# One-row products with the mask and the biases, against the same products over 128 rows

## The chip, the cores and the metric

The kernel runs on one core of one Trainium2 chip, in one launch. The metric is the device time in microseconds (us). Before the change three runs gave 4461.14, 4453.69 and 4463.28 us; their median is 4461.14 us. The cuts that a reader needs of a core are its engines, which run side by side and meet only at semaphores: TensorE (PE in the rows, its weight loads PEld), VectorE (DVE), ScalarE (ACT), GpSimd (POOL) and the DMA queue that SyncE feeds (SP).

## The reference, cut to what matters

The program computes four pairs of an attention and a feed-forward layer on x, of shape (16, 256, 128). The change touches the first attention, to a context of 64 rows a batch, and the routing in front of the experts in the last layer:

```python
# first attention: 16 heads of 64, to the context
sim = einsum(q, k) * scale
sim = where(mask, sim, -max)            # one mask value per batch and context row
x = x + softmax(sim) @ v @ Wout.T + b_out
...
# last layer: the route
route_prob = softmax(xf @ Ws + bs, axis=-1).T     # 8 experts
```

## The kernel before, in words

x is worked on in 32 tiles of 128 tokens, four tiles to a pass, eight passes.

The first attention is `cross_attention` (lines 117 to 469). The weights are folded in pairs first (`fold`, line 235), so that a pass needs, for its two batches, a matrix `g` (scores come straight from the normalised x) and a matrix `vo` (the output comes straight from the probabilities). `unit` (lines 248 and 255) makes these for the next pass, one of eight units per iteration. An iteration `j` is one tile and eight of its 16 heads, 64 in all. Its work on TensorE, in this fixed order: `scores(j)` on lines 270 and 272, a unit for the next pass, on slot 7 also `turn_x` (line 215), `turn_prob(j-2)` on line 282, and `mix(j-3)` on lines 294 and 296. Line 270 puts the mask into the bank of scores as the product of a row of ones and a row of mask values; line 272 adds the scores to it. Line 294, once per tile, puts the bias into the bank of the output in the same way; line 296 adds four products of probabilities and `vo`. Each of these f32 products is two weight loads and two matmuls in the trace, the mask's (bf16) is one of each.

VectorE does, in iteration `i`: `weigh(i-1)` (sum, reciprocal, multiply: lines 360, 361, 364), `soften(i)` (maximum, subtract: 355, 356), and on odd iterations the addition to x and its statistics (368, 371, 372). In slot 3 of a pass it also makes the roots for the next layer (lines 76 to 80), in slot 4 (6 in the first pass) it normalises x for the next pass (347). ScalarE copies the units (437), takes the exponential (447), copies the turned x once a pass (423) and the turned probabilities (443). Everything waits by counting semaphores; no planner is involved.

The route is in `attend_and_route` (lines 3072 to 3360). After the attention of a pass, ScalarE normalises it (`norm`, 3303), TensorE turns it (`turn_r`, 3192), ScalarE copies it (3337), and `route` forms, for each of four tiles, a product with `ws` of eight columns (3200) and adds the bias as a product of a row of ones and the row `bs` (3201). VectorE then lowers and weighs (3269 to 3278) and ScalarE takes the exponential (3341).

Of the kernel before, what the change touches and what calls it, by code (L numbers as in the profile page):

```python
# [16 lines left out]
BF16 = mybir.dt.bfloat16  # L17
# [6 lines left out]
BATCH, SEQ, DIM = 16, 256, 128  # L24
CTX = 64
# [6 lines left out]
GROUP = 8  # L32
# [84 lines left out]
def cross_attention(nc, x_all, ident, dram, s_all):  # L117
# [10 lines left out]
    with ExitStack() as ctx:  # L128
        def sb(name, shape, dt=F32):
            return ctx.enter_context(nc.sbuf_tensor("x_" + name, shape, dt))  # L130
# [3 lines left out]
        def sem(name):  # L134
# [8 lines left out]
        fold_v = sb("fold_v", [128, 2, PAIRS, DIM])  # L143
        b_out = sb("b_out", [1, DIM])
        ctx_t = sb("ctx_t", [128, BATCH * CTX])
        mask_in = sb("mask_in", [1, BATCH * CTX], U8)
        mask_f = sb("mask_f", [1, BATCH * CTX])
        mask_b = sb("mask_b", [1, BATCH, CTX], BF16)
        ones = sb("ones", [1, 128])
        ones_b = sb("ones_b", [1, 128], BF16)  # L150
        stats, mv, var = sb("stats", [128, TILES, 6]), sb("mv", [128, TILES, 2]), sb("var", [128, 3, TILES])
# [12 lines left out]
            sem(n) for n in ("w_k_in", "w_q_in", "ctx_in", "w_v_in", "w_out_in", "b_in", "mask_arrived"))  # L164
        consts, zeroed, mask_made, own_v = sem("consts"), sem("zeroed"), sem("mask_made"), sem("own_vector")
        folded, fold_made, unit_done, unit_made = sem("folded"), sem("fold_made"), sem("unit_done"), sem("unit_made")
# [11 lines left out]
        @block.sync  # L178
        def _(sp):
            def load_x(p):  # L180
                at = slice(PASS_TOK * p, PASS_TOK * p + PASS_TOK)
                sp.dma_start(x_all[:, at], dram["x"][:, at]).then_inc(x_in[p], 16)

            sp.dma_start(w_k[:, :, :], dram["x_Wk"]).then_inc(w_k_in, 16)
            for n in range(2):
                half = slice(64 * n, 64 * n + 64)
                sp.dma_start(w_q[half, :, n, :], dram["x_Wq"][half, :, :]).then_inc(w_q_in, 16)
            load_x(0)
            sp.dma_start(ctx_t[:, :], dram["ctx_t"]).then_inc(ctx_in, 16)
            sp.dma_start(mask_in[:, :], dram["mask"]).then_inc(mask_arrived, 16)  # L190
            sp.dma_start(w_v[:, :, :], dram["x_Wv"]).then_inc(w_v_in, 16)
            for n in range(2):
                half = slice(64 * n, 64 * n + 64)
                sp.dma_start(w_out[half, :, n, :], dram["x_Wout"][half, :, :]).then_inc(w_out_in, 16)
            sp.dma_start(b_out[:, :], dram["x_b"]).then_inc(b_in, 16)
            for p in range(1, PASSES):
                load_x(p)

        @block.gpsimd
        def _(pool):  # L200
            nc.gpsimd.memset(ones[:, :], 1.0).then_inc(consts, 1)
            nc.gpsimd.memset(ones_b[:, :], 1.0).then_inc(consts, 1)
            for w in (w_q, w_out):
                nc.gpsimd.memset(w[0:64, :, 1, :], 0.0).then_inc(zeroed, 1)
                nc.gpsimd.memset(w[64:128, :, 0, :], 0.0).then_inc(zeroed, 1)

        @block.tensor
        def _(pe):
# [49 lines left out]
            def scores(j):  # L258
# [10 lines left out]
                to = score_bank[j % 2]  # L269
                nc.tensor.matmul(to[:, :], ones_b[:, :], mask_b[:, 2 * p + b, :].unsqueeze(1).broadcast_to([1, GROUP, CTX]), start=True, stop=False)  # L270
                at = 128 * (t % PASS_TILES)
# [54 lines left out]
        def _(dve):  # L326
# [57 lines left out]
            dve.wait_ge(mask_made, 2)  # L384
            nc.vector.tensor_copy(mask_b[:, :, :], mask_f[:, :].rearrange("a (b c) -> a b c", c=CTX)).then_inc(mask_made, 1)
            take_stats(1)
# [2685 lines left out]
def attend_and_route(nc, x_all, ident, dram, out, prob, table, weights, w_in, x_kept, table_in, prob_in):  # L3072
# [10 lines left out]
    with ExitStack() as ctx:  # L3083
# [13 lines left out]
        ctx_t, ctx_rows = sb("ctx_t", [128, BATCH * CTX]), sb("ctx_rows", [CTX, BATCH, DIM])  # L3097
        ws, bs, ones = sb("ws", [128, EXPERTS]), sb("bs", [1, EXPERTS]), sb("ones", [1, 128])
        stats, mv = sb("stats", [128, 2, TILES, 6]), sb("mv", [128, 2, TILES, 2])
        var, shift = sb("var", [128, 2, 3, TILES]), sb("shift", [128, 2, TILES])  # L3100
        xn, xn_t = sb("xn", [128, 2, PASS_TOK]), sb("xn_t", [128, 2, PASS_TOK])
        proj_t = sb("proj_t", [128, 2, PASS_TOK])
# [44 lines left out]
        @block.gpsimd  # L3147
        def _(pool):
            nc.gpsimd.memset(ones[:, :], 1.0).then_inc(ones_set, 1)

        @block.tensor
        def _(pe):
# [42 lines left out]
            def route(p):  # L3195
                pe.wait_ge(rn_t_made, p + 1)
                pe.wait_ge(r_lowered, p)
                for t in range(PASS_TILES):
                    s = route_bank[:, EXPERTS * t:EXPERTS * t + EXPERTS]
                    nc.tensor.matmul(s, tile(rn_t[:, p % 2, :], t), ws[:, :], start=True, stop=False)  # L3200
                    last = nc.tensor.matmul(s, ones[:, :], bs[:, :], start=False, stop=True)
                last.then_inc(r_done, 1)

            pe.wait_ge(loaded, 64)
            pe.wait_ge(route_in, 32)
            pe.wait_ge(ones_set, 1)
            for i in range(PASSES + LAG + 1):
# [609 lines left out]
```

## Time and profile before

| | before |
|---|---|
| median of three runs | 4461.14 us |
| the profiled execution's own time | 4456.33 us |
| its span, first to last instruction | 4454.5 us |
| outside the span | 1.8 us |
| PE, DVE, ACT, POOL busy, share of the span | 89%, 80%, 66%, 50% |
| mean granted TensorE clock | 0.931 of full |

The span is from the first to the last instruction of the program. Busy shares are means over stages with different limits: the first attention is the first 309 us, the route a stretch of about 60 us near 4200 us. A matmul's end is modelled, so starts of matmuls are a better ruler than their durations. [...]

### The profile page before, as it was taken

Reading aid. Unit: us, or ns where it says so; the run is one execution under the profiler, and the core shown is the slowest. Engines: PE = TensorE matmul, PEld = TensorE weight load, DVE = VectorE, ACT = ScalarE, POOL = GpSimd, SP = SyncE. Lnnn points to the kernel's source line nnn. Section 1 sums busy time; section 2 is a strip of 40 time slices with the busy share of each in tenths; the row PEclk is TensorE's granted clock in tenths of the full one; section 3 lists DMA queues with packets and bytes.
Section 4 is the critical chain, followed back from the end, with each engine's and each line's share of the span. In section 5 each row is a group of like instructions: output and inputs, shape, how many; then the busy total and the mean of one; then the engine's idle time right before and its main releaser. Section 6 shows DMA issues by size and latency. Waiting matters only on the chain. (4 is left out here: it accounts for less than half of the span.)

```text
span 4454.5 us, 117888 instructions
## 1 busy us (share of the span) xinstructions
PE 3964.2 (89%) x43247; PEld 2386.8 (54%) x43247; DVE 3584.2 (80%) x8496; ACT 2960.2 (66%) x5496; POOL 2206.9 (50%) x1392
## 2 busy tenths in 40 slices
PE   8978999999999999999999999999999855737735
PEld 5644555555555555555555555555555533525534
DVE  6887999899998999989999899989999655356341
ACT  3425787787777777777787787777778545636402
POOL 0005666666666666666666666666666400130006
PEclk9989999999999999999999999999999966868658
DMA  1012232333233332233232332232323200000102
GB/s 43 1 40 65 66 68 64 83 68 69 65 69 82 69 70 65 65 84 70 65 68 64 83 73 64 64 85 65 70 64 68 50 15 12 1 5 18 72 7 37
DMA packets 188120, 251.24 MB, mean 56 GB/s; under 512 B 88676, under 2 KB 129382, under 8 KB 187366
## 3 DMA queue, kind: packets, MB, share of 16 engines
q1 hardware_dynamic: 182054, 240.47, 23.2%
q0 software_dynamic: 5632, 4.33, 0.7%
q8 instruction: 352, 5.77, 0.6%
q14 instruction: 82, 0.67, 0.0%
HBM read 41.65 MB, written 14.30 MB: 13 GB/s over the span
## 5 line engine op out<-in xcount | busy, mean ns | idle before, releaser
L1419 POOL TENSOR_TENSOR f_rot_a<-f_rot_a,f_rot_b 128x1024 f32<-128x1024 f32 x384 | 908.1, 2370 | 311.8 <-DVE f_rot_b L1160 206.6
L1427 POOL TENSOR_TENSOR f_rot_a<-f_rot_a,f_norm 128x1024 f32<-128x1024 f32 x384 | 731.3, 1905 | 648.5 <-DVE f_norm L1178 525.4
L844 PE MATMUL f_bank<-f_w_vo,f_xs_t 128*32 128x512 f32 x6144 | 815.8, 603 | 0.2
L1157 DVE TENSOR_TENSOR f_rot_a<-f_bank,f_rot 128x512 f32<-128x512 f32 x768 | 523.0, 682 | 76.2 <-ACT f_squares L1519 40.4
L1528 ACT ACTIVATE f_vo<-f_bank 128x512 f32<-128x512 f32 x768 | 458.6, 597 | 170.2 <-PE f_bank L844 162.6
L1519 ACT ACTIVATE f_squares<-f_bank 128x512 f32<-128x512 f32 x768 | 455.8, 594 | 113.1 <-PE f_bank L830 67.1
L1540 ACT ACTIVATE f_k_t<-f_bank 64x512 f32<-64x512 f32 x768 | 452.7, 589 | 102.7 <-PE f_bank L866 98.2
L1160 DVE TENSOR_TENSOR f_rot_b<-f_bank,f_rot 128x512 f32<-128x512 f32 x768 | 505.9, 674 | 0.0
L1433 POOL TENSOR_TENSOR f_prob<-f_score,f_stat 128x512 f32<-128x512 f32 x384 | 400.6, 1043 | 192.1 <-DVE f_stat L1210 187.7
L1164 DVE TENSOR_REDUCE f_sums<-f_squares 128x16 f32<-128x1024 f32 x384 | 464.5, 1210 | 4.7 <-ACT f_squares L1519 4.7
L876 PEld LDWEIGHTS f_bank<-f_k_t,f_q_t 128*32 128x32 f32 x12288 | 345.4, 110 | 179.4 <-issue 99.5
L900 PEld LDWEIGHTS f_bank<-f_vo_off,f_prob_t 128*32 128x32 f32 x6144 | 330.8, 110 | 167.3 <-issue 150.7
L830 PE MATMUL f_bank<-f_w_qk,f_xs_t 128*128 128x512 f32 x768 | 400.5, 603 | 22.2 <-DMA f_w_qk<-in_Wqk 7.9
L876 PE MATMUL f_bank<-f_k_t,f_q_t 128*32 128x128 f32 x12288 | 406.0, 273 | 1.2 <-ACT f_bank L1546 0.6
L900 PE MATMUL f_bank<-f_vo_off,f_prob_t 128*32 128x128 f32 x6144 | 406.8, 274 | 0.2
L900 PE MATMUL f_bank<-f_vo,f_prob_t 128*32 128x128 f32 x6144 | 406.8, 274 | 0.0
L836 PE MATMUL f_bank<-f_w_qk,f_xs_t 128*128 128x512 f32 x768 | 401.7, 605 | 0.7 <-DVE f_rot_b L1160 0.7
L1533 ACT ACTIVATE f_q_t<-f_bank 128x512 f32<-128x512 f32 x384 | 227.9, 594 | 260.2 <-PE f_bank L860 260.2
L900 PEld LDWEIGHTS f_bank<-f_vo,f_prob_t 128*32 128x32 f32 x6144 | 330.8, 110 | 0.0
L1206 DVE TENSOR_REDUCE f_stat<-f_score 128x8 f32<-128x512 f32 x384 | 259.9, 677 | 76.8 <-ACT f_score L1550 71.9
L866 PEld LDWEIGHTS f_bank<-ident,f_rot_a 128*128 128x128 f32 x1536 | 180.4, 141 | 217.7 <-issue 153.8
L1198 DVE TENSOR_REDUCE f_stat<-f_bank 128x8 f32<-128x512 f32 x384 | 257.7, 671 | 29.1 <-PE f_bank L876 23.6
(446 smaller groups left out, 7372.8 us busy)
## 6 DMA issues: line engine op xcount, KB each, us to landing
f_vo_off<-f_vo SPq DMA_DIRECT2D x1152, 128.0 KB, 2.3
f_vo_off<-f_vo SPq DMA_DIRECT2D x384, 64.0 KB, 2.0
f_w_qk<-in_Wqk SPq DMA_DIRECT2D x12, 512.0 KB, 5.3
f_vo_dram<-f_vo_pair SPq DMA_DIRECT2D x48, 128.0 KB, 1.8
f_x_shifted<-s_all SPq DMA_DIRECT2D x48, 128.0 KB
f_x_shifted<-s_all SPq DMA_DIRECT2D x48, 127.0 KB
f_w_vo<-f_vo_dram SPq DMA_DIRECT2D x10, 512.0 KB, 5.4
e_w<-in_e_W SPq DMA_DIRECT2D x2, 2048.0 KB, 12.7
```

The costliest lines, as they stand in the source:

```text
L836: nc.tensor.matmul(flat(Q), chunk_x(t), w_qk[:, 0, 512 * g:512 * g + 512], start=True, stop=True).then_inc(q_done, 1)
L844: done = nc.tensor.matmul(bank[V][32 * w:32 * w + 32, :], x[:, at:at + 32], w_vo[:, 4 * g:4 * g + 4, w // 2, :], start=True, stop=True)
L876: done = nc.tensor.matmul(bank[S][32 * w:32 * w + 32, 128 * b:128 * b + 128], q_t[:, g, 128 * b + 32 * w:128 * b + 32 * w + 32], k_t[:, :, ...
L900: done = nc.tensor.matmul(bank[Y][32 * w:32 * w + 32, 0:128], prob_t[:, g, 128 * b + 32 * w:128 * b + 32 * w + 32], source[:, g, 2 * (t % ...
L1157: nc.vector.tensor_tensor(rot_a[:, slot, n, :].rearrange("p (h d) -> p h d", h=GROUP), source, c_tab, ALU.mult)
L1160: nc.vector.tensor_tensor(rot_b[:, g, n, :].rearrange("p (h s d) -> p h s d", h=GROUP, s=2), swapped, s_tab, ALU.mult).then_inc((q_rotated ...
L1164: nc.vector.tensor_reduce(sums[:, g, :], squares[:, g, :, :].rearrange("p n (h d) -> p (n h) d", h=GROUP), AX_X, ALU.add).then_inc(lengths, 1)
L1419: nc.gpsimd.tensor_tensor(rot_a[:, slot, :, :], rot_a[:, slot, :, :], rot_b[:, g, :, :], ALU.add).then_inc(rot_summed, 1)
L1427: nc.gpsimd.tensor_tensor(heads, heads, over(norm[:, 16 * g:16 * g + 16], [128, 16, HEAD_DIM]), ALU.mult).then_inc(qk_normed, 1)
L1519: nc.scalar.activation(squares[:, g, n, :], flat((Q, K)[n]), ACT.Square).then_inc((q_squared, k_squared)[n], 1)
L1528: nc.scalar.activation(vo[:, g, 2 * (t % 2) + j, :], flat(V), ACT.Copy).then_inc((va_copied, vb_copied)[j], 1)
L1540: done = nc.scalar.activation(k_t[r:r + 64, n, 4 * g:4 * g + 4, at:at + 128], flat(T)[r:r + 64, :].rearrange("p (b n) -> p b n", b=4), ACT ...
```

## The change

The stationary row of ones and the moving row (mask, bias) become 128 rows. In the moving operand 127 of them are zero, so the product is the same. The zero rows are written once at the start of each stage, on GpSimd, and three waits are added for them: SyncE's before the load of `b_out`, VectorE's before the mask is cast, and TensorE's at the start of the last stage, which now waits for a copy of `bs` that GpSimd makes after its DMA.

```diff
-        b_out = sb("b_out", [1, DIM])
+        b_out = sb("b_out", [128, DIM])
-        mask_b = sb("mask_b", [1, BATCH, CTX], BF16)
-        ones = sb("ones", [1, 128])
-        ones_b = sb("ones_b", [1, 128], BF16)
+        mask_b = sb("mask_b", [128, BATCH, CTX], BF16)
+        ones = sb("ones", [128, 128])
+        ones_b = sb("ones_b", [128, 128], BF16)
...
-            sp.dma_start(b_out[:, :], dram["x_b"]).then_inc(b_in, 16)
+            sp.wait_ge(cleared, 1)
+            sp.dma_start(b_out[0:1, :], dram["x_b"]).then_inc(b_in, 16)
...
             nc.gpsimd.memset(ones_b[:, :], 1.0).then_inc(consts, 1)
+            pool.wait_ge(consts, 2)
             for w in (w_q, w_out):
                 nc.gpsimd.memset(w[0:64, :, 1, :], 0.0).then_inc(zeroed, 1)
                 nc.gpsimd.memset(w[64:128, :, 0, :], 0.0).then_inc(zeroed, 1)
+            pool.wait_ge(zeroed, 4)
+            nc.gpsimd.memset(b_out[:, :], 0.0).then_inc(cleared, 1)
+            pool.wait_ge(cleared, 1)
+            nc.gpsimd.memset(mask_b[:, :, :], 0.0).then_inc(cleared, 1)
...
-                nc.tensor.matmul(to[:, :], ones_b[:, :], mask_b[:, 2 * p + b, :].unsqueeze(1).broadcast_to([1, GROUP, CTX]), start=True, stop=False)
+                nc.tensor.matmul(to[:, :], ones_b[:, :], mask_b[:, 2 * p + b, :].unsqueeze(1).broadcast_to([128, GROUP, CTX]), start=True, stop=False)
...
+            dve.wait_ge(cleared, 2)
-            nc.vector.tensor_copy(mask_b[:, :, :], mask_f[:, :].rearrange("a (b c) -> a b c", c=CTX)).then_inc(mask_made, 1)
+            nc.vector.tensor_copy(mask_b[0:1, :, :], mask_f[:, :].rearrange("a (b c) -> a b c", c=CTX)).then_inc(mask_made, 1)
...
-        ws, bs, ones = sb("ws", [128, EXPERTS]), sb("bs", [1, EXPERTS]), sb("ones", [1, 128])
+        ws, bs, ones = sb("ws", [128, EXPERTS]), sb("bs", [1, EXPERTS]), sb("ones", [128, 128])
+        bias_rows, bias_set = sb("bias_rows", [128, EXPERTS]), sem("bias_set")
...
             nc.gpsimd.memset(ones[:, :], 1.0).then_inc(ones_set, 1)
+            nc.gpsimd.memset(bias_rows[:, :], 0.0).then_inc(bias_set, 1)
+            pool.wait_ge(bias_set, 1)
+            pool.wait_ge(route_in, 32)
+            nc.gpsimd.tensor_copy(bias_rows[0:1, :], bs[:, :]).then_inc(ones_set, 1)
...
-                    last = nc.tensor.matmul(s, ones[:, :], bs[:, :], start=False, stop=True)
+                    last = nc.tensor.matmul(s, ones[:, :], bias_rows[:, :], start=False, stop=True)
...
-            pe.wait_ge(ones_set, 1)
+            pe.wait_ge(ones_set, 2)
```

## Rows read from the trace of the kernel before

**Rows 1.** Busy time per engine by stage: us, busy (count) each, PEclk, DMA share, GB/s

```profile
0.00:309.00 309.00, 277.96 (x1472) 176.00 (x1472) 247.75 (x648) 118.62 (x209) 5.15 (x14) 0.98 0.06 16
4189.80:4248.40 58.60, 41.84 (x165) 38.71 (x164) 13.99 (x78) 15.23 (x39) 0.00 (x0) 0.50 0.14 45
```

**Rows 2.** VectorE's waits from 80 to 280 us: total us, times, longest

```profile
DVE x_stat L360 <- ACT x_score L447: 11.0, 18, 0.7
DVE x_stat L355 <- PE x_bank L272: 2.7, 11, 0.4
```

**Rows 3.** Timeline of TensorE's matmuls in the first attention: start us, duration us

```profile
273.15 0.63 PE L282 MATMUL x_bank<-ident,x_prob 128*128 128x128 f32 x4
...
275.21 0.38 PE L270 MATMUL x_bank<-x_mask_b,x_ones_b 1*128 1x512 bf16 x1
...
276.82 0.63 PE L282 MATMUL x_bank<-ident,x_prob 128*128 128x128 f32 x4 [0.17 <-ACT x_prob_t L443]
277.28 1.06 PE L296 MATMUL x_bank<-x_vo,x_prob_t 128*128 128x128 f32 x8
278.27 0.39 PE L270 MATMUL x_bank<-x_mask_b,x_ones_b 1*128 1x512 bf16 x1
```

**Rows 4.** The same stretch, weight loads

```profile
273.70 0.29 PEld L294 LDWEIGHTS x_bank<-x_b_out,x_ones 1*128 1x128 f32 x2 [0.17 <-issue]
...
275.52 0.30 PEld L272 LDWEIGHTS x_bank<-x_g,x_xn_t 128*128 128x128 f32 x2 [0.23 <-issue]
...
277.18 0.97 PEld L296 LDWEIGHTS x_bank<-x_vo,x_prob_t 128*128 128x128 f32 x8
```

**Rows 5.** Timeline of matmuls in the third attention, all of 128 rows

```profile
3799.26 0.22 PE L2307 MATMUL a_bank<-a_causal,ident_bf 128*128 128x128 bf16 x1
3799.32 0.75 PE L2306 MATMUL a_bank<-a_k,a_q 128*128 128x256 f32 x2
```

**Rows 6.** Timeline of matmuls at the start of two passes

```profile
235.78 0.38 PE L270 MATMUL x_bank<-x_mask_b,x_ones_b 1*128 1x512 bf16 x1 [0.41 <-ACT x_xn_t L423]
236.10 1.13 PE L272 MATMUL x_bank<-x_g,x_xn_t 128*128 128x512 f32 x2
237.06 0.61 PE L248 MATMUL x_bank<-x_ctx_t,x_fold_q 128*128 128x128 f32 x4
...
268.96 0.39 PE L270 MATMUL x_bank<-x_mask_b,x_ones_b 1*128 1x512 bf16 x1 [0.42 <-ACT x_xn_t L423]
```

**Rows 7.** Timeline about the end of the first pass, TensorE, then VectorE

```profile
63.60 0.66 PE L215 MATMUL x_bank<-ident,x_xn 128*128 128x128 f32 x4 [2.41 <-DVE x_xn L347]
...
70.28 0.69 DVE L355 TENSOR_REDUCE x_stat<-x_bank 128x8 f32<-128x512 f32 x1 [1.51 <-PE x_bank L272]
...
73.13 0.69 DVE L360 TENSOR_REDUCE x_stat<-x_score 128x8 f32<-128x512 f32 x1 [1.44 <-ACT x_score L447]
```

**Rows 8.** Busy time, columns as in Rows 1

```profile
65.50:72.40 6.90, 5.94 (x22) 4.17 (x21) 4.48 (x10) 2.02 (x4) 0.00 (x0) 0.51 0.00 0
```

**Rows 9.** Timeline of VectorE in the last iterations of the first attention

```profile
296.20 0.69 DVE L355 TENSOR_REDUCE x_stat<-x_bank 128x8 f32<-128x512 f32 x1 [1.02 <-PE x_bank L272]
...
307.05 0.29 DVE L368 TENSOR_TENSOR x_all<-x_all,x_bank 128x128 f32<-128x128 f32 x1 [2.08 <-PE x_bank L296]
```

**Rows 10.** VectorE's and ScalarE's waits from 4184 to 4250 us

```profile
DVE y_r_stat L3269 <- PE y_bank L3201: 37.3, 7, 6.4
ACT y_r_score L3341 <- DVE y_r_score L3270: 36.2, 8, 6.9
```

**Rows 11.** Timeline of matmuls in one pass of the route

```profile
4222.39 1.12 PE L3192 MATMUL y_bank<-ident,y_rn 128*128 128x128 f32 x4 [2.31 <-ACT y_rn L3303]
4223.30 0.44 PE L3200 MATMUL y_bank<-y_ws,y_rn_t 128*128 128x8 f32 x2
4223.66 0.59 PE L3201 MATMUL y_bank<-y_bs,y_ones 1*128 1x8 f32 x2
...
4226.80 0.59 PE L3201 MATMUL y_bank<-y_bs,y_ones 1*128 1x8 f32 x2
4229.70 0.69 PE L3192 MATMUL y_bank<-ident,y_rn 128*128 128x128 f32 x2 [2.31 <-ACT y_rn L3303]
```

**Rows 12.** Timeline at the start of the first attention

```profile
13.05 0.95 POOL L205 MEMSET x_w_out<- 64x1024 f32 x1
...
14.93 1.36 SPq L195 DMA_DIRECT2D x_b_out<-in_x_b  x1
...
23.15 0.68 DVE L385 CAST x_mask_b<-x_mask_f 1x1024 bf16<-1x1024 f32 x1
```

**Rows 13.** Timeline at the start of the last attention

```profile
4120.76 1.65 ACT L3303 ACTIVATE y_xn<-x_all,y_shift,y_var 128x128 f32<-128x128 f32 x4 [15.34 <-DMA y_ctx_rows<-in_ctx_rows]
...
4122.66 1.08 PE L3157 MATMUL y_bank<-ident,y_xn 128*128 128x128 f32 x4 [13.35 <-ACT y_xn L3303]
```

More of the change, by code:

```diff
@@ L164, in cross_attention @@
             sem(n) for n in ("w_k_in", "w_q_in", "ctx_in", "w_v_in", "w_out_in", "b_in", "mask_arrived"))
-        consts, zeroed, mask_made, own_v = sem("consts"), sem("zeroed"), sem("mask_made"), sem("own_vector")
+        consts, zeroed, mask_made, own_v, cleared = sem("consts"), sem("zeroed"), sem("mask_made"), sem("own_vector"), sem("cleared")
         folded, fold_made, unit_done, unit_made = sem("folded"), sem("fold_made"), sem("unit_done"), sem("unit_made")
```

## Prediction, on record before the changed kernel ran

> **What bounds the kernel now.** I read the busy time by stage first, since the change touches two stages only: the first attention, 309 us, and the route, 59 us [rows 1]. The reader is to see there that TensorE is the busiest engine in both, and that its granted clock is 0.98 in the one and 0.50 in the other. Busy is not bound, so the waits come next. In the first attention from 80 to 280 us VectorE waits 2.7 us for TensorE's scores and 11.0 us for ScalarE's exponential [rows 2]; the second wait is VectorE's own work coming back (subtract, exponential, sum: at most 0.7 us a time, 18 times), and TensorE has no part in it. TensorE in turn runs without a pause but one of 0.41 or 0.42 us a pass [rows 6]. So both are nearly full, and a pass takes 268.96 - 235.78 = 33.18 us [rows 6]. What a faster TensorE is worth there is what VectorE waits for it, and little more. In the route it is the other way round: VectorE waits 37.3 of 66 us for the last bias product, ScalarE 36.2 us for VectorE [rows 10], and TensorE in turn 2.31 us for ScalarE in a pass of 4229.70 - 4222.39 = 7.31 us [rows 11]. That is one closed chain (normalise, turn, route, lower, exponential, normalise), and whatever TensorE saves in it comes off the time.
>
> **What a one-row product costs.** Starts of matmuls are the ruler. With a bias product between line 282's four matmuls and the next mask product: 275.21 - 273.15 = 2.06 us. Without one: 278.27 - 276.82 = 1.45 us [rows 3]. So its two matmuls of 128 columns cost 0.61 us. Matmuls of 128 rows and 128 columns cost 0.11 us each: line 282's four take 277.28 - 276.82 = 0.46 us. Two would be 0.22 us, so 0.39 us is lost about each bias product. The weight loads show how: the load for line 294 and the one for line 272 behind the mask product both stand behind an idle stretch put down to issue (0.17 and 0.23 us), while line 296's load starts at 277.18, before its first matmul at 277.28 and while line 282's last is still running [rows 3, 4]. A load is hidden behind the matmul before it when both have 128 rows, and it is not when the number of rows changes. The mask product has the same loss: 0.31 us to line 272 (236.10 - 235.78) where 512 bf16 columns at 128 rows would take 4 x (3799.32 - 3799.26 = 0.06), some 0.22 us [rows 5, 6]; 0.10 us ahead of it (278.27 - 277.28 = 0.99 for eight matmuls, against 8 x 0.11); and 0.10 us in line 272, whose two matmuls take 237.06 - 236.10 = 0.96 us where the second alone, with its load hidden, is worth some 0.43. Together 0.30 us. That rows 5 is bf16 between f32 products shows that the type makes no pause.
>
> The saving on TensorE is then 8 x 0.30 + 4 x 0.39 = 3.96 us a pass. In the route six of the seven steps from 4223.30 to 4226.80 are (4226.80 - 4223.66) / 6 = 0.52 us a product. The turn's four cold matmuls take 0.91 us, 0.23 each, and at best the half-speed image of 0.11, 0.21; a product is two [rows 11]. So 0.52 becomes 0.42 to 0.46; I take 0.42, as the first of the four carries an unhidden load: 6 x 0.10 = 0.62 us a pass.
>
> [...]
>
> **The sum, against the profiled execution (4456.33 us, 4454.5 in its span).**
> - Route: eight passes, all in the chain, 8 x 0.62 = 5.0 us (bounds 8 x 0.4 and 8 x 0.7).
> - Steady passes: VectorE's wait for scores, 2.7 us, goes [rows 2]. Behind it VectorE has its own work and ScalarE's exponential, so the rest of the 3.96 us a pass turns into idle time of TensorE.
> - First two iterations: TensorE makes the scores that VectorE waits for, 2 x 0.30 = 0.6 us.
> - End of the first pass: the clock is at 0.51 [rows 8] and VectorE waits 1.51 us for line 272 and 1.44 us for an exponential held up behind a copy from TensorE [rows 7]. The mask product's share of that, at half speed, and the later small waits: 0.9 us.
> - Last pass: VectorE's 1.02 us goes, as a bias and a mask product lie ahead of it at half speed; and one bias product, 0.39 us, lies ahead of the final addition [rows 9]. Together 1.4 us.
>
> Sum 5.0 + 2.7 + 0.6 + 0.9 + 1.4 = 10.6 us.
>
> **What is given back.** TensorE's idle time grows from 0.4 us a pass to 0.42 + 3.96 - 0.52 = 3.9 us. Following the order of work, about 1.1 of it comes where line 296 waits for a copy behind the exponential and 2.3 us in one piece ahead of slot 0, where line 270 waits for the turned x. The trace has one such piece: TensorE idle for 2.41 us before the turn at 63.60, and then the clock at half for 6.9 us [rows 7, 8]. That fall cost VectorE 1.51 + 1.44 - 0.70 = 2.25 us. In the new passes a fall should cost less: TensorE has work from the start, so I take half of those 6.9 us; after 3.4 us at half speed it is 1.7 us late, of which 0.4 to 0.6 is slack, so 1.2 us. [...] Net 10.6 - 3.6 = 7.0 us.
>
> **What costs nothing.** The wider memsets of ones are of the same length per row. The two memsets added at the end of GpSimd's list start at 14.00; the nearest row is 0.95 us for 1024 f32 elements a row, so the larger ends by 15.5 at most, and the cast that waits for it is at 23.15 [rows 12]: cover 7.6 us. Queued behind SyncE's new wait are seven loads of x; it is met near 14.3, ahead of 14.93 when the queue comes to it. Without that cover it would cost at most the memset's 0.95 us, and a gain is excluded, since nothing starts sooner. In the last stage TensorE waits for a copy of eight numbers behind a small DMA issued just after `ctx_rows`, which landed by 4120.76, while TensorE's first matmul is at 4122.66 for ScalarE's sake [rows 13]: 1.9 us of cover. If `bs` landed late, the cost would be that of one small copy, under 0.4 us. I take 0 for all of these.
>
> **The rivals.**
> - Full gain: the clock doesn't fall, as the idle piece is split. For it: it rests at 1.00 through 200 us of passes. Against: the 2.41 us case. 10.6 us less.
> - More than that: zero rows or the shorter pauses keep the clock up at the end of the first pass as well (2 us), or lift it in the route, where the turn and the route take 5.0 of 7.31 us at half speed (4226.80 + 0.59 - 4222.39) and would take about 2 us less a pass [rows 11]. For it: TensorE is packed more densely. Against: half of the route's products have 128 rows already and the clock is 0.50 all through [rows 1]. 13 to 26 us less.
> - No change: the pause isn't set by the rows but by something else about these operands (a new region of memory), and stays. Against: line 282 to line 296 changes operands as well, without a pause [rows 3, 4]. 0 us. [...]
> - Slower: the clock falls in each of the six passes and costs what the first fall cost, 6 x 2.25 = 13.5 us, against a gain of 10.6: 2.9 us more. From five falls of that size it decides the sign.
>
> **How the numbers follow.** Chances: the forecast (one to five falls) 0.48, full gain 0.27, more 0.08, no change 0.10, slower 0.07. Predicted time 4461.14 - 7 = 4454 us. The forecast's own range is a gain of 4.8 to 9.4 us. Medians of three have moved within 10 us among equal runs, so I allow 4 us on either side of a gain of 0 to 14: 4443 to 4463. What a measurement of this kernel can tell from no change is about 0.2%, 8.9 us: the full gain passes it mostly (0.20), the larger always (0.08), the forecast now and then (0.12): faster 0.40. Slower than that needs falls beyond six: 0.04. Same 0.56.
>
> **What would show it.** Right: in the profile after, the step from line 270 to line 272 is 0.21 to 0.22 us, a bias product 0.22 us, a product of the route 0.42 to 0.46, with no idle stretch put down to issue before the loads of lines 272 and 294. VectorE's wait for line 272 in 80 to 280 us is near 0 where the clock is 1.00. TensorE's wait for line 423 is 2 us or more a pass. A pass of the route is 6.7 us. Wrong: unchanged steps (the rows don't matter); a pass of the first attention shorter than 32.6 us (VectorE wasn't the bound); a granted clock of 1.00 in all passes, or below 0.9 in all.

## The result, and the profile after

| | before | after |
|---|---|---|
| median of 20 runs each, in alternation on one chip | 4462.12 us | 4452.5 us |
| ratio after / before, 95% interval | | 0.9979 [0.9973, 0.9986] |
| the profiled execution's own time; its span | 4456.33; 4454.5 us | 4458.58; 4456.8 us |
| first attention, from the first mask product to the last normalised sum | 284.5 us | 277.9 us |
| route, from the first to the last product with `ws` | 56.5 us | 51.8 us |

The changed kernel is faster by 0.21%, with an interval of 0.14% to 0.27%: 6 to 12 us, where the forecast was 7 and 4454 us. One of the 20 executions after took 6802.6 us at a granted clock of 0.551 (a slow state); it is counted in the median and left out of the ratio. The profiled execution happens to be one of its slower ones, so its total says nothing, and its stages have to be compared one by one. The two stages that were changed are 6.7 and 4.7 us shorter. The span is 2.3 us longer all the same, so 13.7 us lie in stages whose instructions are the same. Outside the two stages the profiles of the twelve kernels here show 4113.5 us (the kernel before) to 4127.8 us, and the kernel after stands near the top with 4127.2. Whether the change costs anything there is not shown; the timed runs leave room for about 2 us of it, since the two stages gain 11.4 us and the medians 9.6.

The busy time by stage, with the columns of [rows 1], of the kernel after:

```profile
0.00:309.00 309.00, 247.71 (x1472) 174.15 (x1472) 249.68 (x658) 116.97 (x209) 6.78 (x17) 0.98 0.06 16
4193.50:4248.00 54.50, 36.38 (x165) 34.59 (x164) 14.02 (x78) 15.23 (x39) 0.00 (x0) 0.50 0.16 49
```

TensorE is busy for 30 us less in the first attention, with the same number of matmuls, and no longer leads VectorE. Its mean granted clock stands where it stood, at 0.98 and 0.50. The traces give it as 1.00 or 0.50 (in the kernel before 1.00 from 80 to 280 us, 0.50 from 68.0 to 72.4 us and in the route); a figure between is a mean over a stretch, and half speed below is a granted clock of 0.50. Now the starts of its matmuls, the ruler of the prediction:

```profile
259.87 0.60 PE L288 MATMUL x_bank<-ident,x_prob 128*128 128x128 f32 x4
260.31 0.39 PE L300 MATMUL x_bank<-x_b_out,x_ones 128*128 128x128 f32 x2
260.53 1.06 PE L302 MATMUL x_bank<-x_vo,x_prob_t 128*128 128x128 f32 x8
263.28 0.39 PE L276 MATMUL x_bank<-x_mask_b,x_ones_b 128*128 128x512 bf16 x1 [1.69 <-ACT x_xn_t L430]
263.51 1.02 PE L278 MATMUL x_bank<-x_g,x_xn_t 128*128 128x512 f32 x2
264.37 0.60 PE L288 MATMUL x_bank<-ident,x_prob 128*128 128x128 f32 x4
```

A bias product (line 300, before 294) takes 260.53 - 260.31 = 0.22 us from start to start, where it cost 0.61. A mask product (line 276, before 270) is 0.23 us ahead of its scores here and 0.21 or 0.22 in the other slots, where it was 0.31 to 0.32. The scores take 264.37 - 263.51 = 0.86 us, where they took 0.96 [rows 6]. The weight loads, against [rows 4]:

```profile
265.59 0.10 PEld L276 LDWEIGHTS x_bank<-x_mask_b,x_ones_b 128*128 128x128 bf16 x1
265.70 0.41 PEld L278 LDWEIGHTS x_bank<-x_g,x_xn_t 128*128 128x128 f32 x2
...
267.63 0.30 PEld L300 LDWEIGHTS x_bank<-x_b_out,x_ones 128*128 128x128 f32 x2
267.86 0.97 PEld L302 LDWEIGHTS x_bank<-x_vo,x_prob_t 128*128 128x128 f32 x8
```

Ahead of lines 278 and 302 the idle stretch put down to issue is gone: the load starts while the matmul before it runs (the mask product itself starts at 265.70, and in the same moment the weights of the scores begin to load). The starts of the loads say it for all of them. From 80 to 280 us of the kernel before, a load at a change of rows starts 198 to 203 ns behind the start of the 128-column matmul before it (313 behind the mask product of 512 columns) and 1 to 4 ns ahead of its own matmul; where the rows stay at 128 it starts 1 to 3 ns behind the start of the matmul before it and some 109 ns ahead of its own (medians). After the change the loads of lines 276, 278, 300 and 302 start 2 or 3 ns behind the start of the matmul before them. The waits from 80 to 280 us, against [rows 2]:

```profile
PE x_bank L288 <- ACT x_prob_t L450: 14.3, 16, 1.7
...
DVE x_stat L366 <- ACT x_score L454: 11.0, 18, 0.7
PE x_bank L276 <- ACT x_xn_t L430: 10.2, 6, 1.7
```

VectorE's wait for scores, 2.7 us in 11 pieces, is no longer listed. Its wait for the exponential is 11.0 us in 18 pieces of at most 0.7, as before. What TensorE saved has become its own waiting for ScalarE's two copies. And one pass of the route, against [rows 11], with VectorE's and ScalarE's waits from 4184 to 4250 us [rows 10]:

```profile
4224.93 0.43 PE L3212 MATMUL y_bank<-y_ws,y_rn_t 128*128 128x8 f32 x2
4225.21 0.57 PE L3213 MATMUL y_bank<-y_bias_rows,y_ones 128*128 128x8 f32 x2
4225.64 0.57 PE L3212 MATMUL y_bank<-y_ws,y_rn_t 128*128 128x8 f32 x2
...
4227.77 0.57 PE L3213 MATMUL y_bank<-y_bias_rows,y_ones 128*128 128x8 f32 x2
...
4230.65 1.11 PE L3204 MATMUL y_bank<-ident,y_rn 128*128 128x128 f32 x4 [2.31 <-ACT y_rn L3315]
4231.56 0.43 PE L3212 MATMUL y_bank<-y_ws,y_rn_t 128*128 128x8 f32 x2
```

```profile
DVE y_r_stat L3281 <- PE y_bank L3213: 32.5, 7, 5.7
ACT y_r_score L3353 <- DVE y_r_score L3282: 31.5, 8, 6.9
```

A product takes 0.43 us, a pass 4231.56 - 4224.93 = 6.63 us, and VectorE's and ScalarE's waits have shrunk by 4.8 and 4.7 us, by what the stage became shorter. The 2.31 us that TensorE waits for ScalarE are the same 2.31.

### The profile page after: what moved, and what is told of

Read it like the earlier page. It is cut to its first block and busy times, and to the rows that moved or that the text cites. A ratio compares the mean times of both kernels' runs of the same rounds, so it can differ in the third digit from the quotient of the medians.

```text
span 4456.8 us, 117896 instructions
## 1 busy us (share of the span) xinstructions
PE 3942.4 (88%) x43247; PEld 2391.9 (54%) x43247; DVE 3584.8 (80%) x8496; ACT 2958.5 (66%) x5496; POOL 2208.4 (50%) x1396
```

## The experiments

Medians are of 5 to 11 runs (20 for the kernel after), the kernel before ran in alternation with each on the same chip, and the ratio is to it. Steps are from the start of one matmul to that of the next, medians over many; the pass is that of the steady state.

| kernel | time, before on its chip | ratio, 95% interval | pass, first attention | pass, route |
|---|---|---|---|---|
| before | | | 33.18 us | 7.31 us |
| after | 4452.5, 4462.1 | 0.9979 [0.9973, 0.9986] | 32.55 | 6.63 |
| mask alone | 4456.0, 4461.2 | 0.9990 [0.9981, 0.9999] | 32.53 | 7.31 |
| bias alone | 4458.5, 4461.2 | 0.9995 [0.9986, 1.0004] | 32.78 to 32.80 | 7.31 |
| route alone | 4458.6, 4461.2 | 0.9992 [0.9983, 1.0001] | 33.18 | 6.63 |
| 64 rows | 4461.9, 4461.2 | 1.0002 [0.9993, 1.0011] | 33.18 | 7.31 |
| before, grouped | 4460.2, 4463.7 | 0.9992 [0.9982, 1.0001] | 33.20 | 6.73 |
| no mask | 4459.7, 4468.2 | 0.9981 [0.9972, 0.9990] | 32.51 | 6.64 |
| sums on GpSimd, after | 4462.3, 4468.2 | 0.9983 [0.9974, 0.9992] | 32.34 | 6.63 |
| sums on GpSimd, before | 4468.4, 4468.2 | 1.0002 [0.9993, 1.0011] | 33.00 | 7.31 |
| one bias product | 4447.5, 4468.2 | 0.9955 [0.9941, 0.9968] | 32.55 | 5.36 |
| both additions | 4444.1, 4463.7 | 0.9956 [0.9942, 0.9969] | 32.35 | 5.36 |

**Each part alone.** Three kernels keep all the memory and the waits of the change and differ only in the slices that the products read:

```diff
 mask alone:   ones[0:1, :], b_out[0:1, :]      ones[0:1, :], bias_rows[0:1, :]
 bias alone:   ones_b[0:1, :], mask_b[0:1, ...]  ones[0:1, :], bias_rows[0:1, :]
 route alone:  ones[0:1, :], b_out[0:1, :]      ones_b[0:1, :], mask_b[0:1, ...]
```

> The changed kernel, but only the mask product has 128 rows; the bias product of the first attention and that of the route are made over one row again. My theory (a weight load is hidden behind the matmul before it only when both have the same number of rows; VectorE bounds a steady pass of the first attention, the closed chain through TensorE bounds the route): step mask product to scores 0.215 us instead of 0.31, bias product still 0.6 us, TensorE saves 2.4 us a pass, of which VectorE's wait of 0.52 is worth anything, so a steady pass of 32.6 us as with all edits; the first attention ends 5 us earlier than before; the route's pass stays at 7.31 us. In all 4455 to 4458 against 4462 (ratio 0.9989). Rival (TensorE bounds the first attention, so all its savings come off the time): 8 x 2.4 = 19 us less, 4443.

> The changed kernel, but only the bias product of the first attention has 128 rows. My theory: TensorE saves 4 x 0.39 = 1.56 us a pass; as that is more than VectorE's wait of 0.52, a steady pass is also 32.6 to 32.7 us, so the mask's and the bias's savings overlap rather than add: 3.5 to 4.5 us off the first attention, nothing off the route, 4458 in all (ratio 0.9991). Rival (TensorE bounds): 12.5 us less, and the sum of this run's and the mask run's gains is the gain of the whole first attention.

> The changed kernel, but only the route's bias product has 128 rows. My theory: the first attention as before (pass 33.18 us), a pass of the route 6.64 us instead of 7.31, 5 us off the time: 4457 (ratio 0.9989). Rival (the gain of the whole change lies in the first attention alone): no change, 4462.

With the mask alone the step from line 302 to the mask product falls from 208 to 112 ns, the next from 315 to 216, the one within the scores from 533 to 429: 0.30 us together, as worked out. With the bias alone the steps from the turn through the bias to the second matmul of line 302 fall from 203, 213, 200 and 213 to 112 or less: 0.38 us, where 0.39 was worked out. Read so, each change of the number of rows slows the two matmuls behind it, by about 0.10 us each at a granted clock of 1.00 (three in all for the mask, whose product is a single matmul). In the route, at a granted clock of 0.50, the steps of 291, 235, 287 and 233 all become 213: 0.076 and 0.021 us behind a change, together the 0.10 of the forecast. Each part's stage moves, and the others don't. In the first attention the parts don't add up: 0.65 and 0.40 us a pass alone, 0.63 together. Either edit brings VectorE near its own bound, and the second finds little left. The bias alone was expected at 32.6 to 32.7 us and stays at 32.8, where VectorE still waits for scores, 0.8 us in 5 pieces from 80 to 280 us, at the start of slot 0. The medians are 5.2, 2.6 and 2.6 us under that of before, their sum 10.4, and the whole 9.6. The bias and the route alone gave less than was expected (4 and 5 us); their intervals hold that as well as 1, so the parts are told by their passes.

**How many rows, and how many changes.** Here the products run over 64 rows, 63 of them zero, in the first kernel. The second is the kernel before with the eight products of a pass of the route in another order: four with `ws`, then the four one-row ones. `s(t)` is the slice that was `s`. In that order the output comes out different, by a relative 0.435, so this kernel computes another route; the instructions and their sizes are the same, and only its times are read.

```diff
-last = nc.tensor.matmul(s, ones[:, :], bias_rows[:, :], start=False, stop=True)
+last = nc.tensor.matmul(s, ones[0:64, :], bias_rows[0:64, :], start=False, stop=True)   # the same for mask_b and b_out
```

```diff
 for t in range(PASS_TILES):
-    s = route_bank[:, EXPERTS * t:EXPERTS * t + EXPERTS]
-    nc.tensor.matmul(s, tile(rn_t[:, p % 2, :], t), ws[:, :], start=True, stop=False)
-    last = nc.tensor.matmul(s, ones[:, :], bs[:, :], start=False, stop=True)
+    nc.tensor.matmul(s(t), tile(rn_t[:, p % 2, :], t), ws[:, :], start=True, stop=False, skip_group_check=True)
+for t in range(PASS_TILES):
+    last = nc.tensor.matmul(s(t), ones[:, :], bs[:, :], start=False, stop=True, skip_group_check=True)
```

> The changed kernel with 64 rows of ones, mask and biases instead of 128, in all three places. My theory (the rows must be the neighbour's 128): every pause is back, mask product to scores 0.31 us, a bias product 0.6 us with its neighbours, a product of the route 0.52, pass 33.18 and 7.31 us, time as before, 4460 to 4463 (ratio 1.0000). Rival (a product over one row is slow in itself, or the memory it was read from): as the changed kernel, 0.215 and 0.22 us, pass 32.55 and 6.64, 4452 (ratio 0.9979).

> The kernel before, with one edit: the route of a pass forms its four products with ws first and then its four one-row bias products, where before they took turns. Every one-row product is still there, with its one row; only the number of changes between 128 rows and one falls, from seven within a pass's eight products to one. Theory (a pause of about 0.10 us stands at each change of the number of rows): steps from matmul to matmul of 0.213 us inside both groups, one of 0.29 us between them, and a pass of the route of 7.31 - 6 x 0.10 = 6.73 us or a little less; the whole 4 to 5 us less than before. Rival (each product of one row costs its pause by itself, whatever stands beside it): the pass stays near 7.31 us.

With 64 rows every step is that of one row within 3 ns, in both stages. The timeline of matmuls in a pass of the route, first with 64 rows, then grouped:

```profile
4224.78 0.59 PE L3213 MATMUL y_bank<-y_bias_rows,y_ones 64*128 64x8 f32 x2
4225.31 0.59 PE L3212 MATMUL y_bank<-y_ws,y_rn_t 128*128 128x8 f32 x2
4225.83 0.59 PE L3213 MATMUL y_bank<-y_bias_rows,y_ones 64*128 64x8 f32 x2
```

```profile
4220.70 1.12 PE L3192 MATMUL y_bank<-ident,y_rn 128*128 128x128 f32 x4 [2.31 <-ACT y_rn L3305]
4221.61 1.72 PE L3201 MATMUL y_bank<-y_ws,y_rn_t 128*128 128x8 f32 x8
4223.25 1.87 PE L3203 MATMUL y_bank<-y_bs,y_ones 1*128 1x8 f32 x8
4227.43 1.12 PE L3192 MATMUL y_bank<-ident,y_rn 128*128 128x128 f32 x4 [2.31 <-ACT y_rn L3305]
```

The product over 64 rows and its neighbour over 128 are 0.52 us apart, as with one row [rows 11]. Grouped, the `ws` matmuls take 4223.25 - 4221.61 = 1.64 us (one step of 0.07, six of 0.21, and 0.29 into the first one-row product), and the one-row matmuls among themselves are 213 ns apart, as those over 128 rows, but for the first step behind the change, 236 ns. The pass is 6.73 us, as expected of one change where there were seven; the time came down by 3.5 us, with an interval that holds 1. So a product of one row costs nothing more by itself. What costs is the change of the number of rows from one matmul to the next, here 0.10 us, whether 1 or 64 rows stand between 128. That the operand is a new region of memory, or that its type differs, is ruled out as the cause by the kernel with 64 rows: it reads the same tiles with the same types in the same order as the kernel after, and differs from it in nothing but the rows.

**Which engine bounds a pass now.** Taking the mask products out altogether (so the mask is left out of the scores) takes 8 x 0.21 us more from TensorE's pass. Moving the 32 multiplications that make `s_all` from VectorE to GpSimd takes 4 x 0.34 us from VectorE's; this is done once on the kernel after and once on the one before.

```diff
 no mask:
-nc.tensor.matmul(to[:, :], ones_b[:, :], mask_b[...], start=True, stop=False)
-... x_g, x_xn_t ..., start=False, stop=True).then_inc(scores_done, 1)
+... x_g, x_xn_t ..., start=True, stop=True).then_inc(scores_done, 1)
 sums on GpSimd:
-                if i >= 12 and slot >= 4:
-                    normalise_sum(PASS_TILES * ((i - 12) // PASS_CHUNKS) + slot - 4)
+            for p in range(PASSES):
+                pool.wait_ge(s_rooted, p + 1)
+                for t in range(PASS_TILES * p, PASS_TILES * p + PASS_TILES):
+                    nc.gpsimd.tensor_scalar(s_all[:, DIM * t:DIM * t + DIM], x_tile(t), s_mv[:, t, 0:1], s_var[:, 1, t:t + 1], ALU.subtract, ALU.mult)
```

> The changed kernel without the mask product (the scores start their bank themselves; the mask is left out of the computation). It takes a further 8 x 0.215 = 1.7 us a pass from TensorE. My theory (VectorE, with the exponential it waits for, bounds a steady pass after the change): pass 32.54 us as with the product, time within 1 us of the changed kernel's, 4451 to 4452 (ratio 0.9978). Rival (TensorE still bounds): pass 30.8, time 4440. On the clock: TensorE idles some 7 us a pass; if enough idle time lets the clock fall in the middle passes, it falls here, and the passes with a fall are 1 us longer.

> The changed kernel with the four multiplications a pass that write s_all moved from VectorE to GpSimd, which idles in the first attention. They cost VectorE 0.33 us each, two of them in slots where it would else wait for the exponential, so VectorE's pass is 2 x 0.33 shorter. My theory (VectorE bounds a steady pass after the change): 31.9 us instead of 32.54, 4 to 5 us less in all, 4448 (ratio 0.9968). Rival (TensorE bounds): 32.54, and 4452.

> The same move of s_all to GpSimd in the kernel before the change. My theory: there TensorE is full but for its one wait of 0.42 us a pass, so the pass of 33.18 us can shorten by at most that, to 32.8 or so: 2 to 3 us less, 4459 (ratio 0.9995), against 4 to 5 us in the changed kernel. Rival (the two engines don't limit each other; VectorE alone bounds both kernels): the same 0.66 us a pass as in the changed kernel, pass 32.5, 4456.

Without mask products the pass is 32.51 us against 32.55: 1.7 us less of TensorE is worth 0.04. TensorE does not bound the pass of the kernel after. Less of VectorE is worth 0.21 us there (32.34) and 0.18 before (33.00). VectorE's part in it is real, but the 31.9 us expected were missed by 0.44. VectorE's timeline shows where they are, first in the kernel after, then with the multiplications (line 381) on GpSimd:

```profile
218.79 0.34 DVE L381 TENSOR_SCALAR s_all<-x_all,x_s_mv,x_s_var 128x128 f32<-128x128 f32 x1
219.05 0.68 DVE L366 TENSOR_REDUCE x_stat<-x_score 128x8 f32<-128x512 f32 x1
...
222.57 0.18 DVE L378 BATCH_NORM_AGGREGATE x_s_mv<-x_s_stats 128x2 f32<-128x6 f32 x1
222.67 0.32 DVE L381 TENSOR_SCALAR s_all<-x_all,x_s_mv,x_s_var 128x128 f32<-128x128 f32 x1
222.90 0.68 DVE L366 TENSOR_REDUCE x_stat<-x_score 128x8 f32<-128x512 f32 x1
...
225.78 0.34 DVE L381 TENSOR_SCALAR s_all<-x_all,x_s_mv,x_s_var 128x128 f32<-128x128 f32 x1
226.56 0.69 DVE L366 TENSOR_REDUCE x_stat<-x_score 128x8 f32<-128x512 f32 x1 [0.44 <-ACT x_score L454]
```

```profile
220.10 0.18 DVE L382 BATCH_NORM_AGGREGATE x_s_mv<-x_s_stats 128x2 f32<-128x6 f32 x1
220.24 0.69 DVE L370 TENSOR_REDUCE x_stat<-x_score 128x8 f32<-128x512 f32 x1
...
223.91 0.69 DVE L370 TENSOR_REDUCE x_stat<-x_score 128x8 f32<-128x512 f32 x1 [0.70 <-ACT x_score L454]
...
228.55 0.69 DVE L374 TENSOR_TENSOR x_prob<-x_score,x_stat 128x512 f32<-128x512 f32 x1
229.38 0.69 DVE L365 TENSOR_REDUCE x_stat<-x_bank 128x8 f32<-128x512 f32 x1
```

In slot 6, at 225.78, the multiplication filled a wait for the exponential: the wait is 0.44 us with it and 0.70 without, and nothing is won. In the odd slots it had cost from 222.57 to 222.90, 0.33 us from the aggregate to the sum, where 0.14 is left (220.10 to 220.24): 0.19 each, twice (slots 5 and 7). Only in slot 4, behind line 353, is its whole 0.26 us won. That is 0.64 us a pass. Of this 0.18 goes where VectorE now comes too early for the scores of slot 0 (229.38 - 228.55 = 0.83 us, before 0.65), which wait for the turned x, and 0.14 behind the roots, where a multiplication of VectorE takes 0.81 us instead of 0.69 beside GpSimd's. A further 0.11 goes just ahead of it, from the last of the roots to the next sum (0.31 us in every pass, 0.20 in the kernel after): there stands the added instruction by which VectorE tells GpSimd that the roots are made. That leaves 0.21 us, and 0.21 were measured. In the time the gain does not show: the ratio is 0.9983, that of the kernel after 0.9979, and 4 to 5 us more had been expected. So VectorE with its exponentials bounds a pass, and in slot 0 the chain from `x_xn` by way of TensorE and ScalarE's copy stands close behind it. On the kernel before, TensorE is the second limit at once. From 80 to 270 us VectorE waits for scores more than it did, with less to do (2.6 us in 10 pieces in the kernel before):

```profile
DVE x_stat L359 <- PE x_bank L276: 3.8, 11, 0.4
```

The pass comes down by 0.18 us only, to 33.00, where up to 0.42 had been allowed, and the time does not move. As 0.18 and 0.21 us are nearly alike, it is this wait and not the pass that tells the two kernels apart.

**The clock.** The prediction had the clock fall in three of the six middle passes. After the change it falls in none. The kernel without mask products is the test of this point too, as TensorE has longer idle pieces there. Its timeline, and behind it the windows of its three falls of the granted clock (columns of [rows 1]):

```profile
120.25 0.63 PE L287 MATMUL x_bank<-ident,x_prob 128*128 128x128 f32 x4 [2.53 <-ACT x_prob_t L449]
...
164.35 1.35 PE L277 MATMUL x_bank<-x_g,x_xn_t 128*128 128x512 f32 x2 [1.84 <-ACT x_xn_t L429]
...
218.93 0.63 PE L287 MATMUL x_bank<-ident,x_prob 128*128 128x128 f32 x4 [2.53 <-ACT x_prob_t L449]
```

```profile
120.60:124.00 3.40, 3.40 (x15) 2.54 (x13) 3.23 (x10) 0.85 (x2) 0.00 (x0) 0.52 0.00 0
165.00:168.40 3.40, 3.40 (x16) 2.98 (x15) 2.06 (x3) 0.95 (x2) 0.00 (x0) 0.52 0.00 0
219.60:223.00 3.40, 3.40 (x12) 1.96 (x10) 3.26 (x9) 1.11 (x2) 0.00 (x0) 0.52 0.01 2
```

In the kernel after, the two pieces of a pass are 1.50 us (ahead of `turn_prob`) and 1.69 us (ahead of the mask product), and the clock is 1.00 from 80 to 280 us. So it is in the profiles of the mask alone, the bias alone, one bias product, sums on GpSimd and both additions. Without mask products the first piece is 2.53 us, and three falls appear in the same stretch, half speed for 3.4 us each. They don't cost alike: VectorE's passes there are 32.51, 32.50, 32.65, 33.54, 32.51 and 32.51 us. Two falls cost nothing: VectorE is busy for 3.2 of the 3.4 us in them. The one at 165.0, in slot 0, where there is no slack, costs 0.14 us in the one pass and 0.83 in the next, 1.0 us (the other 0.2 of 33.54 stands in slot 2, where the kernel after has it too, in a pass of 32.74 us without a fall). The forecast's price of a fall, 1.2 us, was a little more than that of the dearest place. The lower clock of the kernel without mask products is not that of one execution: its means are 0.925 to 0.928 in 11 executions, those of the kernel before on the same chip 0.927 to 0.932. Why two of the five pieces of 2.53 us brought a fall and three did not, and one of the 1.84 us pieces did, stays open, and so does whether it is the size of the pieces that decides or their sum in a pass, as this kernel changes both.

**What more there is to have.** The bias is the same for all tiles, so one product of 32 columns can open the bank for all four tiles of the route. The second kernel here adds the sums on GpSimd to it.

```diff
+nc.tensor.matmul(route_bank[:, 0:EXPERTS * PASS_TILES], ones[:, :], bias_rows[:, :].unsqueeze(1).broadcast_to([128, PASS_TILES, EXPERTS]), start=True, stop=False)
 for t in range(PASS_TILES):
-    nc.tensor.matmul(s, tile(rn_t[:, p % 2, :], t), ws[:, :], start=True, stop=False)
-    last = nc.tensor.matmul(s, ones[:, :], bias_rows[:, :], start=False, stop=True)
+    last = nc.tensor.matmul(s, tile(rn_t[:, p % 2, :], t), ws[:, :], start=False, stop=t == PASS_TILES - 1)
```

> The changed kernel with one bias product of 32 columns for the four tiles of a route's pass, ahead of the four products with ws, in place of four bias products of 8 columns. The closed chain through TensorE bounds the route, and a product there costs its two weight loads, 2 x 0.213 us, whatever its columns: three products less are 1.28 us a pass, so 5.36 us instead of 6.64, and 8 x 1.28 = 10 us less than the changed kernel: 4442 (ratio 0.9956). Rival (after the change the chain is bound by ScalarE's and VectorE's part, TensorE has slack): pass 6.64, time 4452.

> The changed kernel with two further edits together: one bias product over all four tiles of the route in place of four, and the multiplications for the next layer moved from VectorE to GpSimd in the first attention. Theory (the two stages don't touch each other): the pass of the route 5.36 us and that of the first attention 32.34 us, each as with the edit alone, and the time 20.7 us (one bias product alone) plus about 1.5 us less than before, a ratio near 0.995. Rival (what is saved early comes back as a wait for DMA at the start of a later stage): the passes are as said but the time is that of one bias product alone or more.

```profile
4213.61 1.12 PE L3204 MATMUL y_bank<-ident,y_rn 128*128 128x128 f32 x4 [2.31 <-ACT y_rn L3315]
4214.52 0.48 PE L3210 MATMUL y_bank<-y_bias_rows,y_ones 128*128 128x32 f32 x2
4214.81 1.85 PE L3213 MATMUL y_bank<-y_ws,y_rn_t 128*128 128x8 f32 x8
4218.97 1.12 PE L3204 MATMUL y_bank<-ident,y_rn 128*128 128x128 f32 x4 [2.31 <-ACT y_rn L3315]
```

The pass of the route is 5.36 us, 1.27 less than after: three products of 0.43 us, taken out of the same closed chain with the same 2.31 us of waiting. The first product behind the turn takes 0.29 us with its 32 columns (4214.81 - 4214.52), where that of the kernel after takes 0.28 with 8 (4225.21 - 4224.93); the matmuls with `ws` behind it and their loads start 213 ns apart, and the turn's, of 128 columns, 214 (medians). The kernel is 20.7 us under that of before on its chip, at 0.9955, and its interval lies clear of that of the kernel after. The sums on GpSimd, added to it, show in the passes (32.35 us) and not in the time: 0.9956 on another chip. That is what the rival foresaw, but the interval is 6 us wide to either side and the gain looked for 1.5 us, so it decides nothing. Nor do the profiles: outside the two stages the one with both additions is 2.2 us longer than that of one bias product alone, well within what such profiles differ by.

## Why the prediction was right, and where it was not

- **A load is hidden only between matmuls of the same number of rows.** Right, and shown for 1, 64 and 128 rows: by the steps, by the starts of the loads (2 or 3 ns behind the start of the matmul before them, where behind one of 128 columns they stood 198 to 203), by 64 rows, and by the grouped order. Why a change of rows holds a load back, the runs don't show. The durations of the loads say little of it: in the route before their medians are 0.31 us over one row and 0.33 over 128.
- **The prices.** 0.30 us for a mask product, right to 0.01. 0.10 us for a product of the route, right (0.52 to 0.43).
- **The route, 5.0 us.** Measured 4.7. From one pass's first `ws` product to the next's the first saves 0.77 us and the others 0.67 or 0.68, but for the second, which is 8.33 us where it was 8.32; what holds that one was not looked into. The chain otherwise is as described.
- **VectorE bounds a steady pass after.** Right: the exponential's wait is unchanged, and a TensorE with 1.7 us less a pass brings 0.04. But the size was off: 2.7 us in six passes were taken from the wait for scores, and the passes became 0.63 us shorter each, 3.6 us from the second to the seventh with one longer pass among them. VectorE's idle time in a pass fell by 0.51 us (33.19 - 29.32 before, 32.54 - 29.18 after), close to the 2.7 / 6; its busy time fell by 0.14, which the sum had not counted. The prediction said that a pass below 32.6 us would speak against VectorE as the bound; at 32.55 it did so by its letter, and that test was drawn too narrowly around a term that was too small. TensorE's wait for the turned x, 1.69 us, is also short of the 2 us or more that it named as a sign of being right.
- **First two iterations and end of the first pass, 0.6 + 0.9 us.** Measured 2.9: 0.2 up to the first maximum, 1.64 in the first pass and 1.73 in the second, less the steady 0.63. The 1.51 and 1.44 us of [rows 7] went as a whole, not by the mask product's share. The clock did fall here, but for half as long, and VectorE had no wait left but the usual one. Most of this is the clock: see the kernel with the route alone, below. TensorE's matmul behind its pause, in the timeline, and the stretch of half speed, as busy time with the columns of [rows 1]:

```profile
63.79 1.11 PE L221 MATMUL x_bank<-ident,x_xn 128*128 128x128 f32 x4 [3.38 <-DVE x_xn L353]
```

```profile
63.60:66.90 3.30, 3.11 (x15) 3.12 (x16) 3.16 (x8) 0.25 (x1) 0.00 (x0) 0.51 0.03 5
```

  And VectorE's maximum and sum that answer to the later two of [rows 7]:

```profile
69.11 0.69 DVE L361 TENSOR_REDUCE x_stat<-x_bank 128x8 f32<-128x512 f32 x1
...
71.22 0.69 DVE L366 TENSOR_REDUCE x_stat<-x_score 128x8 f32<-128x512 f32 x1 [0.69 <-ACT x_score L454]
```

  Half speed for 3.3 us where it was 6.9 [rows 8]: this is one place of the prediction's rival of a larger gain. What the fall is worth is told by the kernel with the route alone, whose first attention has the steps of the kernel before, and whose clock stays at 1.00 here behind the same pause:

```profile
64.19 0.66 PE L221 MATMUL x_bank<-ident,x_xn 128*128 128x128 f32 x4 [2.42 <-DVE x_xn L353]
```

  Its first two passes are 40.95 and 33.19 us, where the kernel before has 42.12 and 34.27: the fall of 6.9 us costs 1.17 + 1.08 = 2.25 us. Among the five profiles with the old steps it is there in four, for 6.8 or 6.9 us; among the four with all of the change (after, sums on GpSimd, one bias product, both additions) it lasts 3.4 us in three and is absent in one, and the first pass is 40.48 or 40.49 us in all four. So the change seems to halve the fall and takes its whole price away, but by luck of the execution there may be nothing to take. Without the fall the term would be 0.7 us, below the 1.5 of the forecast.
- **Last pass, 1.4 us.** Measured 0.1. Up to the last maximum 1.29 us are won (270.44 to 299.88 before, 264.57 to 292.72 after); here too most is the clock, as the kernel with 64 rows, with the old steps but half as long a fall, takes 28.39 us for it where before took 29.44 and after 28.15. And 1.17 are given back behind it, where a second fall of the clock (0.66 from 295 to 300 us) meets the two last additions:

```profile
297.94 0.29 DVE L374 TENSOR_TENSOR x_all<-x_all,x_bank 128x128 f32<-128x128 f32 x1 [1.29 <-PE x_bank L302]
...
301.06 0.29 DVE L374 TENSOR_TENSOR x_all<-x_all,x_bank 128x128 f32<-128x128 f32 x1 [2.29 <-PE x_bank L302]
```

- **The clock takes back 3.6 us.** This is the step that failed: nothing was taken back in the middle passes, whose granted clock is 1.00 throughout, which the prediction itself had named as a sign of being wrong. The 3.6 us were three falls of 1.2 us in six passes, an estimate that no run shows: the kernel after had no fall there, and the three of the kernel without mask products cost 1.0 us together. The reason given was an idle stretch of TensorE of 2.3 us in one piece ahead of slot 0. The total was right: 32.54 - 29.02 us busy = 3.5 us a pass against 3.9. But where line 288 waits, 1.50 us stood and not 1.1, and ahead of slot 0 1.69 and not 2.3. Pieces of that size brought no fall in the middle passes of any profile; with one of 2.53 us there were three, in the kernel without mask products. Falls of this kind exist, and the change stops short of them. How much idle time brings one, no run shows: behind the same 2.41 and 2.42 us at the end of the first pass the clock fell in one kernel and not in the other.
- **What should cost nothing** cost nothing: the cast that waits for the zeroed rows starts at 23.16 us, before at 23.15. The wider memsets of `ones` and `ones_b` take 0.20 us each, those of one row took 0.19 and 0.20. In the last stage GpSimd's copy of `bs` takes 0.18 us and ends at 4122.10, and TensorE's first matmul starts at 4123.49, released by ScalarE.

The sum before anything was given back was 10.6 us. The stages show 6.7 + 4.7 = 11.4, and the timed runs 9.4 (0.21% of 4462). So the net 7.0 was too low, mostly by what the clock was wrongly charged for, and the rival of the full gain, 10.6 us, came nearer than the likeliest case. That 10.6 came near the measured gain is in part luck: the steady passes gave 3.6 us where 2.7 were summed, the last pass 0.1 where 1.4 were, and the end of the first pass gave its 2.9 by way of the clock. The time, 4452.5 us, lies in the range, but the range of 4443 to 4463 held the unchanged time too. The prediction gave 0.56 to a change that a measurement could not tell from none; with 20 runs of each it was told.

## What to carry to other kernels

Where short products of a few rows stand between products of 128, fill their rows with zeros, or group them: what cost time here was each change of the number of rows, not the product (0.30 and 0.39 us for the two changes about a mask and a bias product in the first attention, 0.10 us for one in the route). Count such changes in the starts of matmuls, since durations hardly show them: the median of a bias matmul in the route went from 0.37 to 0.36 us, the step of a product from 0.52 to 0.43. Then ask who bounds the stage: in the closed chain of the route the 0.67 or 0.68 us saved in TensorE's products came off each steady pass whole, while in the first attention, where VectorE was nearly as full, 3.8 us a pass less of TensorE's busy time gave 0.63. And before a gain is charged for a falling clock, look how the idle time will be cut into pieces.

## What was not expected of the hardware

- 64 rows between 128 cost what one row does: 291 and 288 ns a step in the route against 291 and 287. One-row matmuls behind each other are 213 ns apart at half speed, as those of 128 rows. A change of rows slows two matmuls behind it, not one.
- A fall of the clock for 3.4 us costs between nothing and 1.0 us, by its place in the pass; one of 6.9 us at the end of the first pass cost 2.25 us. Behind the same pause of 2.4 us it came in one kernel and not in another with the same steps.
- A multiplication on VectorE of 128x512 took 0.81 us beside one of GpSimd, and 0.69 without, once in each steady pass.
- A single product of 32 columns for four tiles (0.29 us from start to start) replaced four of 0.43.
